# Softmax sums beside the values of an attention: two heads' values and ones in one stationary block, 32x32 transposes on VectorE, and another order of the streams

## The chip, the cores and the metric

The kernel runs on one core of a Trainium2 chip. The metric is the device time of one execution in microseconds; less is better. All data is float32.

## The reference, cut to what matters

Four transformer blocks are applied to `x` of shape (128, 64, 128): 128 batch elements, 64 tokens, 128 features. They hold five attentions with 16 heads of 8 features each, two MLPs and a last block with a router and three experts. The change touches only the attentions, whose core is:

```python
attn = jnp.einsum('bhnd,bhsd->bhns', q, k) * SCALE
attn = jax.nn.softmax(attn, axis=-1)
o = jnp.einsum('bhns,bhsd->bhnd', attn, v)      # 64 queries, 64 keys, 16 heads of 8
```

## The kernel before, in words

**Tiling.** Four batch elements make a group (`GROUP`), so there are 32 groups. Each group passes through all five attentions, which makes 160 attentions in a run. Five groups are in flight at a time, one in each stream (`STREAMS = 5`).

**What sets the order.** The steps of one group stand in `GROUP_STEPS`. The string `SEQUENCE` says, digit by digit, which stream makes its next step; `interleave()` turns it into `ORDER`. Every engine walks through the same `ORDER` and issues its own part of each step, in that order. Semaphores tie the engines together.

**Steps of an attention.** `q`, `k` and `v` are projections. `tops` computes scores once to find maxima, `lows` transposes the negated maxima, `scores` computes the scores again less the maximum. ScalarE takes the exponential of each of the four banks of scores (L1203, one for each `g`). The result is `pT[s]`, laid out as keys of two heads (64 partitions each) by (`g`, batch element `tb`, `lo`, query). `g` runs over four quads of heads.

**Sums and values on TensorE.** For `sums` (L874) a stationary block of ones and zeros with 32 columns, `own_ones`, adds up the exponentials over the keys. Each matmul has 256 moving columns, and there are 8 of them. For `values` (L887) the stationary block holds the values, and there are 32 matmuls of 64 moving columns. Both use a quarter of the array's columns for a matmul. Which quarter (strip) it is follows from the 32 partitions of the bank that the output goes to, `dst[QUAD * g:QUAD * (g + 1), ...]`. In both steps `g` is the innermost loop:

```python
for tb in range(GROUP):
    for lo in range(2):
        for g in range(TURNS):
            mm = nc.tensor.matmul(dst[QUAD * g:QUAD * (g + 1), tb * SEQ:(tb + 1) * SEQ], ...
```

The trace has two rows for each such float32 matmul, which are called passes here, and one or two for each weight load.

**On VectorE.** `sums` is inverted over all 128x256 elements (L1063). `values` is then multiplied by it (L1070) into `oT`, which the step `out` (L897) projects.

**Another step that the prediction speaks of.** `l3_evidence` (L945) makes two matmuls on rows 0 to 63 of the array and then two on rows 64 to 127. Its loop over the halves is the outer one.

**Banks.** Four PSUM banks form a ring that all projections, sums and values share. A step takes the next bank and waits until its last content has been moved out. The other four banks (`turns`) belong to `tops` and `scores`.

Of the kernel before, what the change touches and what calls it, by code (L numbers as in the profile page):

```python
# [7 lines left out]
ALU = mybir.AluOpType  # L8
# [6 lines left out]
D = 128  # L15
# [66 lines left out]
ALL_WEIGHTS = 16 * (3 + len(W_LOADS[1:]))  # L82
# [48 lines left out]
def attention(a):  # L131


    return [("q", a), ("k", a), ("v", a), ("tops", None), ("lows", None), ("scores", None),
            ("sums", None), ("values", None), ("out", a)]
# [6 lines left out]
def norm(eps, how):  # L142
# [26 lines left out]
    "0021100003030101012012311010100102000030112001100100111100100231000120000100101110312002110201201010"  # L169
    "0200210122012131012022100120200102021011012201032112312003230002213212302133202031230310321303024031"  # L170
    "0410301441203320203411101032132132443421143201143213401232244200302344230043320310041241134203120012"
    "4412232424012312033143420234413303224011042121003404103104032024013003210432434041431411143234234120"
    "1034332024031130241021413024012401214024431143230242003143201031044032431340320121423211434041422210"
    "3423043231241432201130322303241421430400220112340221143230132223300244011234043214101241040420103314"
    "3202433042311040412144340023210134110223101434210313242043401340313021203302403104103014412033202034"
    "1110103213213244342114320114321340123224420030234423004332031004124113420312001244122324240123120331"
    "4342023441330322401104212100340410310403202401300321043243404143141114323423412010343320240311302410"
    "2141302401240121402443114323024200314320103104403243134032012142321143404142221034230432312414322011"
    "3032230324142143040022011234022114323013222330024401123404321410124104042010331432024330423110404121"
    "4434002321013411022310143421031324204340134031302120330240310410301441203320203411101032132132443421"  # L180
    "1432011432134012322442003023442300433203100412411342031200124412232424012312033143420234413303224011"
    "0421210034041031040320240130032104324340414314111432342341201034332024031130241021413024012401214024"
    "4311432302420031432010310440324313403201214232114340414222103423043231241432201130322303241421430400"
    "2201123402211432301322233002440112340432141012410404201033143202433042311040412144340023210134110223"
    "1014342103132420434013403130212033024031041030144120332020341110103213213244342114320114321340123224"
    "4200302344230043320310041241134203120012441223242401231203314342023441330322401104212100340410310403"
    "2024013003210432434041431411143234234120103433202403113024102141302401240121402443114323024200314320"
    "1031044032431340320121423211434041422210342304323124143220113032230324142143040022011234022114323013"
    "2223300244011234043214101241040420103314320243304231104041214434002321013411022310143421031324204340"
    "1340313021203302403104103014412033202034111010321321324434211432011432134012322442003023442300433203"  # L190
    "1004124113420312001244122324240123120331434202344133032240110421210034041031040320240130032104324340"
    "4143141114323423412010343320240311302410214130240124012140244311432302420031432010310440324313403201"
    "2142321143404142221034230432312414322011303223032414214304002201123402211432301322233002440112340432"
    "1410124104042010331432024330423110404121443400232101341102231014342103132420434013403130212033402014"
    "3043041210131212314310221001424304123140020101300241003023401310342310224312413421343321431204340320"
    "4142033124403231021420320421432414112002430344033021340434210043030324211104203124140130423300231403"
    "4103110304403140341110041421201420441240213414132031042410304111404021424300401413240221143310410413"
    "1040112311102011241143014132034100401240110400101301420130411214001343401041403303110011130041111310"
    "104010310404311420301441101031410141100104120110341414401101311111113011"
# [15 lines left out]
def bank_uses(kind, arg):  # L215
# [5 lines left out]
        "lows": (0, 1), "sums": (1, 0), "values": (1, 0),  # L221
# [127 lines left out]
def build(nc, x, cond, context, weights, biases, rows, ident_in, own_head_in, own_ones_in, gate_store, out):  # L349
# [3 lines left out]
    with ExitStack() as ctx:  # L353
# [16 lines left out]
        own_ones = sb("own_ones_sb", [D, 2, QUAD])  # L370
# [22 lines left out]

        v_heads = each("v_heads", [D, GROUP * TURNS, 2 * QUAD])
        top = each("top", [D, D])
        inv_sum = each("inv_sum", [D, TOK])
        low = [i[:, 0:D] for i in inv_sum]
        oT = each("oT", [D, GROUP, SEQ])

# [132 lines left out]
        with nc.Block() as block:  # L532
# [23 lines left out]
            def _(pool):  # L556
# [3 lines left out]
                for s in range(STREAMS):  # L560

                    nc.gpsimd.memset(v_heads[s][:, :, :], 0.0).then_inc(consts_made, 1)
# [729 lines left out]
```

## Time and profile before

| | us |
|---|---|
| median of 3 runs | 2047.76 (2044.34 to 2049.5) |
| profiled execution, its own time | 2036.93 |
| span of the profiled execution | 2035.2 |
| TensorE (PE) busy | 1920.9 |
| weight loads (PEld) busy | 1591.5 |
| VectorE (DVE) busy | 1685.4 |
| ScalarE (ACT) busy | 1411.7 |
| GpSimd (POOL) busy | 648.7 |

The profiled execution is 10.8 us below the median of the runs. 1.7 us of it lie outside the span. Busy times of engines overlap each other, so they do not add up. Busy time of TensorE is the union of its passes, each of which has a modelled end.

### The profile page before, as it was taken

To read this page: it belongs to the slowest core of one execution; us is meant where nothing else is said; L and a number is where in the kernel's file an instruction comes from. 1 tells how busy PE (TensorE), PEld (TensorE's weight loads), DVE (VectorE), ACT (ScalarE), POOL (GpSimd) and SP (SyncE) were. 2 spreads that over 40 slices of the span, in tenths; PEclk is the share of its full clock that TensorE was granted. 3 is DMA by queue.
4 is the path that set the end of the run, shared out by engine and by line. 5 is a ranking of instruction groups with operands and counts; after the bars stand their busy time and mean duration, and the time that the engine had idled before them with its cause. 6 is when DMAs were issued, how large, how long until landed. Compare 5 with 4: busy or idle time off the path is not lost.

```text
span 2035.2 us, 93251 instructions
## 1 busy us (share of the span) xinstructions
PE 1920.9 (94%) x40741; PEld 1591.5 (78%) x40741; DVE 1685.4 (83%) x3915; ACT 1411.7 (69%) x3672; POOL 648.7 (32%) x1132
## 2 busy tenths in 40 slices
PE   3789999999999999999999999999999999999998
PEld 2567878887877887878887877887888887777877
DVE  2778888888888898878898888898888888889875
ACT  1455767777776777776777776777776777676777
POOL 1322333333333323333323333333333332323322
PEclk9899999999999999999999999999999999999999
DMA  4200000000000000000000000000000000000000
GB/s 176 53 3 3 16 21 21 21 11 18 21 16 21 21 21 11 19 16 21 21 20 10 20 16 21 21 21 21 9 16 21 21 21 8 21 16 8 3 3 14
DMA packets 48113, 42.97 MB, mean 21 GB/s; under 512 B 12640, under 2 KB 38368, under 8 KB 47456
## 3 DMA queue, kind: packets, MB, share of 16 engines
q1 hardware_dynamic: 47712, 37.02, 6.4%
q8 instruction: 326, 5.34, 1.1%
q14 instruction: 75, 0.61, 0.1%
HBM read 32.54 MB, written 4.46 MB: 18 GB/s over the span
## 4 chain that ended last, share of the span: by engine, by line
PE 79%; DVE 10%; ACT 6%; issue 2%; DMA 1%; POOL 0%; DVEq 0%; ACTq 0%; POOLq 0%
PE bank L967 9%; PE turns L858 8%; PE turns L841 7%; PE turns L862 7%; PE bank L874 6%; PE bank L887 6%; PE bank L904 5%; PE bank L914 5%; PE bank L976 4%; PE bank L897 3%; PE bank L812 3%; PE bank L779 3%; DVE top L1059 3%; PE bank L827 3%; PE bank L816 3%; ACT pT L1203 2%
## 5 line engine op out<-in xcount | busy, mean ns | idle before, releaser
L1203 ACT ACTIVATE pT<-turns 128x512 f32<-128x512 f32 x640 | 330.2, 602 | 165.1 <-PE turns L862 164.7
L738 POOL TENSOR_TENSOR shifted<-moments,eps 128x2 f32<-128x2 f32 x256 | 50.1, 196 | 1127.1 <-DVE moments L1023 1126.5
L1059 DVE TENSOR_REDUCE top<-turns 128x32 f32<-128x2048 f32 x160 | 364.2, 2276 | 44.3 <-PE turns L841 43.6
L1063 DVE RECIPROCAL inv_sum<-bank 128x256 f32<-128x256 f32 x160 | 279.7, 1748 | 39.7 <-PE bank L874 38.6
L858 PE MATMUL turns<-inv_sum,of_keys 32*128 32x128 f32 x5120 | 277.9, 284 | 3.8 <-issue 2.3
L862 PE MATMUL turns<-q_heads,k_heads 32*128 32x128 f32 x5120 | 263.0, 271 | 2.7 <-issue 2.6
L1238 ACT ACTIVATE pT<-bank,mod 128x64 f32<-128x64 f32 x896 | 195.7, 331 | 51.7 <-PE bank L967 50.6
L858 PEld LDWEIGHTS turns<-inv_sum,of_keys 32*128 32x128 f32 x5120 | 206.8, 187 | 30.5 <-ACT inv_sum L1152 13.1
L862 PEld LDWEIGHTS turns<-q_heads,k_heads 32*128 32x128 f32 x5120 | 209.2, 187 | 4.0 <-issue 3.8
L1029 DVE TENSOR_SCALAR n_rows<-x_rows,moments,rstd 128x128 f32<-128x128 f32 x512 | 185.6, 405 | 29.3 <-POOL rstd L740 28.2
L841 PE MATMUL turns<-k_heads,q_heads 32*128 32x128 f32 x5120 | 189.4, 283 | 12.5 <-ACT pT L1203 10.2
L1180 ACT ACTIVATE k_heads<-bank,key_bias,own_head_sb 128x256 f32<-128x256 f32 x320 | 164.3, 573 | 51.2 <-PE bank L816 51.1
L740 POOL TENSOR_TENSOR rstd<-shifted,minus_halves 128x2 f32<-128x2 f32 x256 | 187.1, 731 | 20.1
L887 PEld LDWEIGHTS bank<-pT,v_heads 128*32 128x32 f32 x10240 | 161.9, 110 | 36.6 <-issue 16.1
L841 PEld LDWEIGHTS turns<-k_heads,q_heads 32*128 32x128 f32 x5120 | 159.2, 186 | 39.6 <-issue 26.8
L1051 DVE TENSOR_SCALAR q_heads<-bank,b_sb,own_head_sb 128x256 f32<-128x256 f32 x320 | 156.5, 530 | 34.9 <-PE bank L812 34.4
L887 PE MATMUL bank<-pT,v_heads 128*32 128x64 f32 x10240 | 177.4, 220 | 8.0 <-issue 6.4
L874 PE MATMUL bank<-pT,own_ones_sb 128*32 128x256 f32 x2560 | 170.8, 383 | 4.9 <-ACT pT L1203 4.7
L1190 ACT ACTIVATE v_heads<-bank 64x128 f32<-64x128 f32 x640 | 138.6, 267 | 21.5 <-PE bank L827 19.2
L967 PE MATMUL bank<-nT,w_sb 128*128 128x256 f32 x448 | 137.2, 387 | 0.3 <-issue 0.3
L904 PE MATMUL bank<-nT,w_sb 128*128 128x256 f32 x512 | 135.3, 392 | 0.2
L1152 ACT ACTIVATE inv_sum<-bank 128x128 f32<-128x128 f32 x160 | 46.2, 289 | 126.8 <-PE bank L849 126.3
(150 smaller groups left out, 3923.1 us busy)
## 6 DMA issues: line engine op xcount, KB each, us to landing
gates<-gate_store SPq DMA_DIRECT2D x64, 256.0 KB, 4.2
x_rows<-x SPq DMA_DIRECT2D x32, 128.0 KB, 2.1
c_rows<-context SPq DMA_DIRECT2D x32, 128.0 KB, 2.1
out<-x_rows SPq DMA_DIRECT2D x32, 128.0 KB, 1.8
w_sb<-weights SPq DMA_DIRECT2D x1, 2368.0 KB, 12.6
pT<-weights SPq DMA_DIRECT2D x1, 1024.0 KB, 4.9
logit_bias<-logit_store SPq DMA_DIRECT2D x64, 1.5 KB, 3.4
row_sb<-rows SPq DMA_DIRECT2D x1, 769.5 KB, 6.7
```

What stands on the lines that cost most here:

```text
L740: nc.gpsimd.tensor_tensor(rstd[s][:, :], shifted[s][:, :], minus_halves[:, 0, :], ALU.pow).then_inc(rstd_in[s], 1)
L841: mm = nc.tensor.matmul(by_turn[g][:, tb * D:(tb + 1) * D], q_heads[s][part, tb, :, :], k_heads[s][part, tb, :, :], start=True, stop=True)
L858: nc.tensor.matmul(by_turn[g][:, tb * D:(tb + 1) * D], of_keys[part, 2 * tb:2 * tb + 2, :], low[s][part, :], start=True, stop=False)
L862: mm = nc.tensor.matmul(by_turn[g][:, tb * D:(tb + 1) * D], k_heads[s][part, tb, :, :], q_heads[s][part, tb, :, :], start=False, stop=True)
L874: mm = nc.tensor.matmul(dst[QUAD * g:QUAD * (g + 1), 0:TOK], own_ones[:, lo, :], pT[s][:, g, :, lo, :], start=lo == 0, stop=lo == 1)
L887: mm = nc.tensor.matmul(dst[QUAD * g:QUAD * (g + 1), tb * SEQ:(tb + 1) * SEQ], v_heads[s][:, tb * TURNS + g, lo * QUAD:(lo + 1) * QUAD], p ...
L904: mm = nc.tensor.matmul(dst[:, c * TOK:(c + 1) * TOK], w(layer["w1"], 0, 2 * half + c), nT[s][:, :, :], start=True, stop=True)
L967: mm = nc.tensor.matmul(dst[:, r * TOK:(r + 1) * TOK], weight, src[:, :, :], start=c == 0, stop=c == 1)
L1059: nc.vector.tensor_reduce(top[s][:, :].rearrange("p (g c) -> p g c", c=32)[:, :, 0:2 * GROUP], turns[:, :, :].rearrange("p g (c k) -> p g ...
L1063: nc.vector.reciprocal(inv_sum[s][:, :], banks.take()[:, 0:TOK]).then_inc(v_emptied, 1)
L1203: nc.scalar.activation(turn_cols[s][:, g, :], by_turn[g][:, :], ACT.Exp, scale=ATT_SCALE).then_inc(scores_read, 1)
L1238: m = nc.scalar.activation(dst, src[:, at], ACT.Silu, bias=mod[s][:, k, tb:tb + 1])
```

## The change

1. `sums` is gone as a step. The stationary block of `values` gets 32 columns for two heads: 8 columns of values of the first head, 8 of the second, 8 of ones on the first head's keys and 8 of ones on the second's. So a matmul gives values and sums. It no longer accumulates over `lo`; the output fills all 512 columns of a bank.
2. The loop over `g` becomes the outermost loop of `values`. It waits at each `g` for that exponential alone.
3. VectorE transposes the bank in 32x32 blocks, which brings queries to the partitions. It inverts 32 sums for each partition, multiplies 128x256, and transposes back.
4. ScalarE moves the values out of the bank in two instructions of 64x256 instead of four of 64x128. Columns of two masks change places for that, and `wv` is read in another order.
5. Ten memsets on GpSimd write the ones at the start; the load of `own_ones` is gone. The transposed rows are kept in `q_heads`.
6. `SEQUENCE` is another string of digits, with one step less for each attention.

```diff
@@ TensorE, steps of ORDER
-                    if kind == "sums":
-
-                        after("pT", s)
-                        dst = to_v.slot()
-                        for lo in range(2):
-                            for g in range(TURNS):
-                                mm = nc.tensor.matmul(dst[QUAD * g:QUAD * (g + 1), 0:TOK], own_ones[:, lo, :], pT[s][:, g, :, lo, :],
-                                                      start=lo == 0, stop=lo == 1)
-                        mm.then_inc(v_filled, 1)
+                    if kind == "values":
+
+                        after("v", s)
+                        dst = to_v.slot()[:, :].rearrange("p (b h l q) -> p b h l q", b=GROUP, h=2, l=2)
+                        for g in range(TURNS):
+                            pe.wait_ge(scores_read, ready["pT", s] + g + 1)
+                            for tb in range(GROUP):
+                                for lo in range(2):
+                                    mm = nc.tensor.matmul(dst[QUAD * g:QUAD * (g + 1), tb, :, lo, :], v_heads[s][:, 2 * (tb * TURNS + g) + lo, :],
+                                                          pT[s][:, g, tb, lo, :].rearrange("p (h q) -> p h q", h=2), start=True, stop=True)
                         mm.then_inc(v_filled, 1)
-                    if kind == "values":
-
-                        after("v", s)
-                        after("pT", s)
-                        dst = to_v.slot()
-                        ready["o", s] = to_v.moved_out()
-                        for tb in range(GROUP):
-                            for lo in range(2):
-                                for g in range(TURNS):
-                                    mm = nc.tensor.matmul(dst[QUAD * g:QUAD * (g + 1), tb * SEQ:(tb + 1) * SEQ],
-                                                          v_heads[s][:, tb * TURNS + g, lo * QUAD:(lo + 1) * QUAD], pT[s][:, g, tb, lo, :],
-                                                          start=lo == 0, stop=lo == 1)
-                        mm.then_inc(v_filled, 1)
@@ VectorE
-                    if kind == "sums":
-                        nc.vector.reciprocal(inv_sum[s][:, :], banks.take()[:, 0:TOK]).then_inc(v_emptied, 1)
-                        sums_at[s] = banks.uses
-
                     if kind == "values":
 
-                        src = banks.take()
-                        dve.wait_ge(v_emptied, sums_at[s])
-                        nc.vector.tensor_tensor(oT[s][:, :, :].rearrange("p g q -> p (g q)"), src[:, 0:TOK], inv_sum[s][:, :],
-                                                ALU.mult).then_inc(v_emptied, 1)
+                        nc.vector.transpose(weighed[s], banks.take()[:, :]).then_inc(v_emptied, 1)
+                        dve.wait_ge(v_emptied, banks.uses)
+                        by_query = weighed[s].rearrange("p (n c) -> p n c", c=4 * HD)
+                        own_result(nc.vector.reciprocal(inv_sum[s][:, :, :], by_query[:, :, 2 * HD:4 * HD:HD]))
+                        own_result(nc.vector.tensor_tensor(o_rows[s][:, :].rearrange("p (n a d) -> p n a d", a=2, d=HD),
+                                                           by_query[:, :, 0:2 * HD].rearrange("p n (a d) -> p n a d", a=2),
+                                                           inv_sum[s][:, :, :].unsqueeze(3).broadcast_to([D, GROUP * 4, 2, HD]), ALU.mult))
+                        nc.vector.transpose(oT[s][:, :, :].rearrange("p g q -> p (g q)"), o_rows[s][:, :]).then_inc(o_turned, 1)
@@ ScalarE
-                            for lo in range(2):
-                                at = lo * QUAD + (2 * pair + lo) * HD
-                                m = nc.scalar.activation(v_heads[s][part, :, at:at + HD],
-                                                         src[part, 0:TOK].rearrange("p (n l d) -> p n l d", l=2, d=HD)[:, :, lo, :],
-                                                         ACT.Identity)
+                            m = nc.scalar.activation(v_heads[s][part, :, HD * pair:HD * (pair + 1)],
+                                                     src[part, 0:TOK].rearrange("p (n d) -> p n d", d=HD), ACT.Identity)
@@ the order of the streams, first line of many
-    "0021100003030101012012311010100102000030112001100100111100100231000120000100101110312002110201201010"
+    "0101000002201010130311101002201130320030012001101010111200100310001300200100101101021102012010010200"
```

On TensorE, in the middle of the program, sums and values of one attention stand as two rows before, here one behind the other (L827 is a `v`, L841 a `tops`, L904 an MLP step):

```order
L904 MATMUL bank<-nT,w_sb 128x256 x2
L827 MATMUL bank<-w_sb,nT 32x64 x16
L874 MATMUL bank<-pT,own_ones_sb 32x256 x8
L887 MATMUL bank<-pT,v_heads 32x64 x32
L841 MATMUL turns<-k_heads,q_heads 128x128 x16
```

After the change TensorE has one row of 32 matmuls (L882), and five rows of other streams until the projection of this attention's result (L893):

```order
L882 MATMUL bank<-pT,v_heads 32x2x32 x32
L833 MATMUL bank<-w_sb,cT 32x64 x16
L847 MATMUL turns<-k_heads,q_heads 128x128 x16
L785 MATMUL bank<-ident_sb,n_rows 128x128 x2
L916 MATMUL bank<-nT,w_sb 128x256
L893 MATMUL bank<-w_sb,oT 128x128 x2
```

The eight matmuls of `own_ones` are gone; the 32 matmuls of the values are as many and as wide as they were (2x32 columns are 64), but their order by strip is that of the new loop.

On VectorE, in the middle of the program, before the change an attention of stream 2 has its inversion and its product with another stream's work between them:

```order
L1063 RECIPROCAL inv_sum2<-bank3 128x256
L1029 TENSOR_SCALAR n_rows3<-x_rows3,moments3,rstd3 128x128 x2
L1070 TENSOR_TENSOR oT2<-bank1,inv_sum2 128x256
```

After it, an attention of stream 0 has four instructions in a row, each of which needs the one before it:

```order
L1055 TENSOR_REDUCE top1<-turns 128x4x8
L1060 STREAM_TRANSPOSE q_heads0<-bank3 128x512
L1063 RECIPROCAL inv_sum0<-q_heads0 128x32
L1064 TENSOR_TENSOR o_rows0<-q_heads0,inv_sum0 128x256
L1067 STREAM_TRANSPOSE oT0<-o_rows0 128x256
```

Two instructions became four, and the wait for them lies in one piece.

## Rows read from the trace of the kernel before

**Rows 1.** The page's busy times: engine, us, share of the span, instructions.
```profile
PE 1920.9 (94%) x40741; PEld 1591.5 (78%) x40741; DVE 1685.4 (83%) x3915; ACT 1411.7 (69%) x3672; POOL 648.7 (32%) x1132
PEclk9899999999999999999999999999999999999999
```

**Rows 2.** The page's chain that ended last, by engine.
```profile
PE 79%; DVE 10%; ACT 6%; issue 2%; DMA 1%; POOL 0%; DVEq 0%; ACTq 0%; POOLq 0%
```

**Rows 3.** Stretches: us, busy time of PE, PEld, DVE, ACT, POOL; clock, DMA.
```profile
500.00:1000.00 500.00, 485.06 (x10508) 404.30 (x10504) 426.43 (x990) 363.98 (x942) 163.21 (x285) 1.00 0.07 18
1000.00:1500.00 500.00, 486.12 (x10547) 404.18 (x10545) 431.25 (x1000) 361.18 (x940) 167.76 (x292) 1.00 0.07 19
```

**Rows 4.** The chain in order of time: start us, us, what, passes.
```profile
1003.56 1.03 PE bank L887 x64
...
1016.43 1.00 PE bank L874 x16
1017.44 0.89 PE bank L887 x64
...
1020.76 0.45 PE bank L897 x4
...
1022.52 0.58 PE bank L827 x32
1023.11 0.86 PE bank L874 x16
1023.97 0.89 PE bank L887 x64
1024.86 1.10 PE turns L841 x32
```

**Rows 5.** Groups by line on PE: passes, busy us, mean ns, idle before.
```profile
L887 PE MATMUL bank<-pT,v_heads 128*32 128x64 f32 x10240 | 177.4, 220 | 8.0 <-issue 6.4 <-DVE inv_sum L1063 1.5
L874 PE MATMUL bank<-pT,own_ones_sb 128*32 128x256 f32 x2560 | 170.8, 383 | 4.9 <-ACT pT L1203 4.7
```

**Rows 6.** L945's first passes: stretches, PE busy (passes in it), PEld busy.
```profile
1001.40:1001.42 0.02, 0.01 (x1) 0.01 (x1) 1.00 0.00 0
1001.42:1001.43 0.01, 0.01 (x2) 0.01 (x2) 1.00 0.00 0
1001.56:1001.58 0.02, 0.02 (x3) 0.02 (x4) 1.00 0.00 0
1001.58:1001.60 0.02, 0.02 (x4) 0.02 (x4) 1.00 0.00 0
```

**Rows 7.** Timeline around 1001 to 1008 us: start, us, instruction, what ended the idle time.
```profile
1001.41 0.67 PE L945 MATMUL bank<-pT,c_rows 64*128 64x64 f32 x8
1002.10 0.45 ACT L1152 ACTIVATE pT<-bank 128x128 f32<-128x128 f32 x2 [0.42 <-PE bank L945]
...
1007.86 2.06 ACT L1203 ACTIVATE pT<-turns 128x512 f32<-128x512 f32 x4 [3.99 <-PE turns L862]
```

**Rows 8.** Groups by line on DVE: count, busy us, mean ns, idle before.
```profile
L1059 DVE TENSOR_REDUCE top<-turns 128x32 f32<-128x2048 f32 x160 | 364.2, 2276 | 44.3 <-PE turns L841 43.6
L1063 DVE RECIPROCAL inv_sum<-bank 128x256 f32<-128x256 f32 x160 | 279.7, 1748 | 39.7 <-PE bank L874 38.6
L1037 DVE TENSOR_TENSOR nT<-nT,mod 128x256 f32<-128x256 f32 x160 | 82.2, 514 | 5.5
L1070 DVE TENSOR_TENSOR oT<-bank,inv_sum 128x256 f32<-128x256 f32 x160 | 67.1, 419 | 20.0 <-PE bank L887 12.3 <-issue 0.2
L1116 DVE RECIPROCAL inv_r<-total_r 128x2 f32<-128x2 f32 x32 | 5.3, 166 | 1.1
L629 DVE COPY of_keys<-own_row 128x512 f32<-128x512 f32 x1 | 0.4, 427 | 0.0
```

**Rows 9.** Groups by line on ACT: count, busy us, mean ns, idle before.
```profile
L1190 ACT ACTIVATE v_heads<-bank 64x128 f32<-64x128 f32 x640 | 138.6, 267 | 21.5 <-PE bank L827 19.2
L1152 ACT ACTIVATE nT<-bank 128x256 f32<-128x256 f32 x64 | 24.7, 386 | 24.5 <-PE bank L779 23.7
```

**Rows 10.** Timeline of GpSimd at the start: start, us, instruction.
```profile
0.82 4.50 POOL L562 MEMSET v_heads<- 128x1024 f32 x5
46.92 0.19 POOL L738 TENSOR_TENSOR shifted<-moments,eps 128x2 f32<-128x2 f32 x1 [41.60 <-DVE moments L1023]
```

More of the change, by code:

```diff
@@ L134, in attention @@
     return [("q", a), ("k", a), ("v", a), ("tops", None), ("lows", None), ("scores", None),
-            ("sums", None), ("values", None), ("out", a)]
+            ("values", None), ("out", a)]
 def mlp(m):
@@ L174 @@
[L174 to L183, printed above, removed]
@@ new lines @@
+    "2440230124013403014421423204122321400142222014003341142034041322321340313132441434321210430143313002"
+    "4012124410041213430233023121013310114432033104143242201240043024324131402001433220410211203224403203"
+    "4201134414203231224341044301423100322144034421204113120433021401024031213203004104301214032214312314"
+    "4134231130001343240400244112203402341132031021243230210012103242433431013120430234203340021104140311"
+    "1431204031022403240231240412342332042334103201320114303244023012401340301442142320412232140014222201"
@@ L200 @@
+    "111001111111"
 )
@@ L220, in bank_uses @@
         "kvnorm": (1, 0) if modulated else (0, 1), "q": (1, 0), "k": (0, 1), "v": (0, 1),
-        "lows": (0, 1), "sums": (1, 0), "values": (1, 0),
+        "lows": (0, 1), "values": (1, 0),
         "out": (1, 0), "fc1": (0, 1), "fc2": (1, 0), "l3_query": (0, 1), "l3_scores": (1, 0),
@@ L392, in build @@
         q_heads, k_heads = each("q_heads", [D, GROUP, 2, SEQ]), each("k_heads", [D, GROUP, 2, SEQ])
-        v_heads = each("v_heads", [D, GROUP * TURNS, 2 * QUAD])
+        v_heads = each("v_heads", [D, GROUP * TURNS * 2, 4 * HD])
         top = each("top", [D, D])
-        inv_sum = each("inv_sum", [D, TOK])
-        low = [i[:, 0:D] for i in inv_sum]
+        o_rows = each("o_rows", [D, TOK])
+        inv_sum = each("inv_sum", [D, GROUP * 4, 2])
+        low = [o[:, 0:D] for o in o_rows]
+        weighed = [q[:, :, :, :].rearrange("p g l q -> p (g l q)") for q in q_heads]
         oT = each("oT", [D, GROUP, SEQ])
@@ L414, in build @@
         top3, total3, inv3 = each("top3", [D, 2]), each("total3", [D, 2]), each("inv3", [D, 2])
-        p3 = [i[:, 0:D].rearrange("p (t k) -> p t k", t=2) for i in inv_sum]
-        pn3 = [i[:, D:2 * D].rearrange("p (t k) -> p t k", t=2) for i in inv_sum]
+        p3 = [o[:, 0:D].rearrange("p (t k) -> p t k", t=2) for o in o_rows]
+        pn3 = [o[:, D:2 * D].rearrange("p (t k) -> p t k", t=2) for o in o_rows]
         p3T = in_turns(3, TOK, 2, SEQ)
@@ L562, in _ @@
                     nc.gpsimd.memset(v_heads[s][:, :, :], 0.0).then_inc(consts_made, 1)
+                for s in range(STREAMS):
+                    pool.wait_ge(consts_made, 3 + STREAMS + 2 * s)
+                    for pair in range(2):
+                        at = HD * (2 + pair)
+                        nc.gpsimd.memset(v_heads[s][SEQ * pair:SEQ * (pair + 1), :, at:at + HD], 1.0).then_inc(consts_made, 1)
             @block.tensor
@@ L990, in _ @@
                 count = Counted(dve)
-                banks, sums_at, attended = Emptier(dve, ring, FOR_VECTOR, v_filled), {}, 0
+                banks, attended = Emptier(dve, ring, FOR_VECTOR, v_filled), 0
                 def own_result(ins):
```

60 lines of the change are left out of this document (32 added, 28 removed).

## The prediction

> **What bounds the kernel now.** I read the busy times first. TensorE is busy for 1920.9 of 2035.2 us, VectorE for 1685.4 and ScalarE for 1411.7 [rows 1]. The chain that ended last then says who holds the end: 79% of it is TensorE's own work, VectorE has 10% and ScalarE 6% [rows 2]. Last I read stretches in the middle. In 500 us TensorE is busy for 485 to 486 and VectorE for 426 to 431, at a granted clock of 1.00, which is the upper level, 2.4 GHz [rows 3]. So TensorE stands idle for about 15 us in 500, some 60 us in the run without its start. The reader is to see that the program is bound by what TensorE has to do: an edit counts by the TensorE time that it adds or takes, and nothing else can give back more than those 60 us.
>
> **The sums go.** On the chain, where TensorE never stops, the step L874 takes 0.86 us (once) and 1.00 us (where the next step is of another kind) [rows 4]. I take 0.93 us. 160 attentions give 149 us less. Bounds: 138 and 160 us.
>
> **The values keep their count and change their order.** This is the term that decides. The 32 matmuls leave 64 passes, before as after. Before, the 64 passes take 0.89 us on the chain [rows 4], while one of them alone lasts 220 ns in the records [rows 5]; so many of them overlap. How many count as simultaneous is read from the pace. A pass of 128 columns over the whole array takes 0.45/4 = 0.112 us (L897) [rows 4], so 64 columns take 0.056 us. 0.89 us are 16 times 0.056 us. So each strip works through its own 16 passes at the pace of the whole array, and the four strips do so at the same time. The sums agree: 4 passes of 256 columns a strip, 4 x 0.224 = 0.90 us against 0.86 [rows 4].
>
> The new loop gives TensorE all 16 passes of strip 0, then all 16 of strip 1, and so on. Two passes of one strip cannot share it. If the strips took turns entirely, the step would last 64 x 0.056 = 3.56 us. What helps is that TensorE can let a pass overtake earlier ones that wait for another part of the array. How far it does that is seen at one place only, L945. Its code has four passes on the lower rows and then four on the upper. The rows show a second pass begun by 1001.43, and the third only at 1001.56 to 1001.58 [rows 6]. With passes of 64 columns on one half 0.056 us apart at least, the second one started belongs to the other half: it overtook three passes (and their weight loads) that stood before it. Both results also came out together: ScalarE, waiting for L945, moved both at 1002.10, after all eight passes of 0.67 us [rows 7]. So overtaking reaches three passes or more, and nothing in the trace shows how many more.
>
> With an overtaking of n passes the next strip starts when n passes of the present one are left to begin. The step then has 64 - 3n passes one after another, as long as n is at most about 10. n = 3 gives 55 passes, 3.06 us; n = 0 gives 3.56 us; n = 16 or more lets two whole strips run side by side, 1.78 us, and without any limit it is 0.89 us as before. I take n = 4, next to the only row: 52 passes, 2.89 us, which is 2.00 us more than now, 320 us in 160 attentions. I choose a small n because three is what is seen, and each further pass that stands aside needs room for itself and its load.
>
> The Trainium skill bears on this, in "TensorE: Matmul & The Clock Gate", Part 3, "The mechanism". It says that matmuls start and end strictly in the order of the program; only weight loads are pulled ahead. By that rule n is 0, and the sum would be 80 us above mine or more. The row on L945 speaks against it: there a matmul started before three earlier ones. The same section also speaks of a reorder window that is 64 deep. Counted in loads and matmuls this would be two strips of this step; nothing in these rows shows such a depth.
>
> **The new waits on TensorE.** `values` waits for one exponential at a time. The four of them last 2.06 us together [rows 7], 0.52 us each, and a strip takes 0.67 us (12 passes) or more; so once the first is there the later ones come in time. Behind the waiting instruction stand all streams' matmuls. Before, the same step waited for all four, and ahead of L887 only 8.0 us were idle in the run [rows 5]. I cost this at nothing; the old wait covers it.
>
> **VectorE.** Gone: 1748 + 419 ns [rows 8]. New: a transpose of 128x512 out of a bank, not shown by any row. The nearest rows are the copy of 128x512, 427 ns, and the reduction over 2048 columns of banks, 2276 ns or 1.11 ns a column, so 570 ns; as bounds I keep 0.43 us and, at the slowest pace of any row (the inversion, 6.8 ns a column), 3.5 us. I take 0.65 us. The inversion of 32 columns: (1748 - 166)/254 = 6.2 ns a column on top of 166 ns, so 0.35 us. The product with its broadcast operand is between 419 and 514 ns, I take 0.45. The transpose back of 128x256 I take at 0.40 us (bounds 0.3 and 1.75). Together 1.85 us against 2.17: VectorE is relieved by 0.3 us an attention, 51 us in all, down from 1685. It isn't the bound, so the sum gets nothing for that. On the transposes, the Trainium skill, "Vector Engine (DVE) Microarchitecture Reference", 3.8, gives one element a cycle for each lane, by which 512 columns would be an estimate of 0.53 us; no row here shows it.
>
> The path from the last pass of the values to `out` grows from 0.42 to about 1.9 us. In the rows of the new order a `v`, a `tops`, two transposes and a matmul of the experts stand between them: 0.58 + 1.10 us for the first two alone [rows 4], and more than 0.4 us for the rest. That hides it there; where less lies between, TensorE waits for up to 1 us.
>
> **The rest.** ScalarE's four moves of 267 ns become two of at most 386 ns [rows 9]: 0.3 us less, off the path. The added memsets follow five that end at 5.3 us, while GpSimd has nothing to do until 46.9 us [rows 10]; even 5 us of them would be hidden. One small load less before the start: nothing.
>
> **The idle time.** TensorE gets more work, VectorE and ScalarE less, and each attention has one step, one bank use and one change of array layout less. Of the 60 us some are given back; I take 20 (bounds 0 and 60). A worse stream order could cost as much.
>
> **Sum.** 2036.93 (profiled execution) - 149 + 320 - 20 = 2188 us. The median of the runs before lies 10.8 us above the profiled one, so 2199 us; I say 2198.
>
> **The rivals.**
> *Deep overtaking (ends faster).* TensorE lets a strip overtake 16 passes or more. Two strips at a time: 1.78 us a step, 160 x 0.89 = 142 more, 149 less, 20 given back: 2010, or 2021 as a median. All four at a time: 0.89 us, which gives 1868 and 1879. For it: the overtaking is real, and it is the same machine that keeps four strips full now. Against it: only three passes are shown. It decides from a step of 0.89 + 0.93 + 20/160 = 1.95 us, 35 passes, n of about 10. Chance 0.29. The reorder window of 64 in the skill's page is its sentence.
> *Strict order between strips.* n = 0: 3.56 us, 160 x 2.67 - 149 - 20 = +258, so 2306. Rows 6 speak against it. Chance 0.08. The skill's rule on strict order is its sentence.
> *VectorE late.* The transposes cost near their upper bound, or the longer path to `out` is not covered. If half of the attentions make TensorE wait for 1 us, 80 us come on top of the forecast: 2278. If a transpose of 128x512 took 3.5 us and one of 128x256 1.75, VectorE would need 6.05 us an attention instead of 2.17, 1685 + 620 = 2305 us, and be the bound. Chance 0.05.
> *The forecast* (n from 3 to about 7): 0.58, its own range 2110 to 2265.
>
> **How the numbers follow.** Slower by over 0.3% (about what a measurement of this kernel can tell from no change): 0.58 + 0.08 + 0.05 = 0.71, less 0.02 for a forecast whose n and idle time fall out so well that nothing is lost: 0.69. Of the deep rival's 0.29, 0.26 end faster and 0.03 within 0.3%, which makes 0.05 there. The range must leave out 2 in 10 at most: it takes the forecast's own range and goes down to two strips at a time, 1995 to 2268; outside are overtaking of all strips and strict order.
>
> **What would show it.** In the trace after: the values step (L882 x64) on the chain for about 2.9 us instead of 0.89, its busy time near 160 x 3.05 = 490 us, TensorE's busy share at 95% or more, VectorE at about 1630 us. If the step shows 1.8 us or less, the overtaking was mis-sized and the kernel is at par or faster. If it shows 3.5 us, there is none between strips. If VectorE is busy beyond 1900 us, or `out` waits for `oT` for more than 40 us in all, the VectorE part was wrong.

## The result, and the profile after

The changed kernel takes 2252.59 us, the median of 4 runs (2248.81 to 2257.74). The kernel before took 2046.5 us on the same chip (2044.34 to 2049.5). The ratio is 1.1008, with a 95% interval from 1.098 to 1.1035. The forecast was 2198 us. The profiled span grew from 2035.2 to 2249.8 us, by 214.6 us.

The page of the kernel after: busy times, granted clock, the chain that ended last by engine and by line. It answers to [rows 1, 2].

```profile
PE 2116.3 (94%) x38181; PEld 1847.0 (82%) x38181; DVE 1666.7 (74%) x4235; ACT 1400.8 (62%) x3346; POOL 655.2 (29%) x1142
...
PEclk8899999999999999999999999999999999999999
...
PE 80%; DVE 10%; ACT 5%; issue 2%; POOL 0%; DMA 0%; SPq 0%; ACTq 0%; DVEq 0%
PE bank L882 22%; PE bank L963 8%; PE turns L864 7%; PE turns L847 6%; PE turns L868 6%; PE bank L910 5%; PE bank L900 4%; PE bank L972 4%; DVE top L1055 4%; PE bank L818 3%; PE bank L822 3%; PE bank L785 3%; PE bank L893 3%; PE bank L833 3%; ACT pT L1196 2%
```

TensorE has 2560 passes less than before and is busy for 195 us more. VectorE and ScalarE are busy for less. The chain's shares by engine are within a point of those of before, and its first line is the values step, L882. So the bound is still TensorE, and one step of it became dear.

The groups of the kernel after by line, on PE and on DVE: passes or instructions, busy us, mean ns of one, idle time before them. They answer to [rows 5, 8].

```profile
L882 PE MATMUL bank<-pT,v_heads 128*32 128x64 f32 x10240 | 508.1, 220 | 0.5 <-ACT pT L1196 0.4
...
L1067 DVE STREAM_TRANSPOSE oT<-o_rows 128x256 f32<-128x256 f32 x160 | 71.3, 445 | 5.5
...
L1064 DVE TENSOR_TENSOR o_rows<-q_heads,inv_sum 128x256 f32<-128x256 f32 x160 | 70.8, 442 | 5.5
...
L1060 DVE STREAM_TRANSPOSE q_heads<-bank 128x512 f32<-128x512 f32 x160 | 114.7, 717 | 284.2 <-PE bank L882 284.2
...
L1063 DVE RECIPROCAL inv_sum<-q_heads 128x32 f32<-128x32 f32 x160 | 56.5, 353 | 5.4
```

The values had 177.4 us of TensorE before and have 508.1 now, with the same 10,240 passes of the same 220 ns. Only fewer of them overlap. VectorE waits 284.2 us for them, which costs nothing.

The chain in order of time shows one such step, and the one behind it (start, us, what, passes). It answers to [rows 4].

```profile
1013.30 0.43 PE bank L822 x2
1013.74 2.94 PE bank L882 x61
1016.68 0.04 PE bank L833 x3
1016.72 0.01 PE bank L882
1016.73 0.04 PE bank L833 x3
1016.78 0.01 PE bank L882
1016.79 0.04 PE bank L833 x3
1016.83 0.01 PE bank L882
1016.85 0.45 PE bank L833 x23
1017.29 1.92 PE bank L900 x8
```

61 passes take 2.94 us where 64 took 0.89 to 1.03 [rows 4]. The end shows the overtaking itself. L833 is the `v` of another stream, on all four strips. Three of its passes, on the free strips, start ahead of the third-last pass of L882, three more ahead of the second-last, and three more ahead of the last.

Four stretches that begin just ahead of this step show when its strips start. They count L882 alone; the number behind the first x is that of its passes begun so far:

```profile
1013.60:1014.35 0.75, 0.69 (x12) 0.69 (x13) 1.00 0.09 23
1013.60:1014.37 0.77, 0.70 (x14) 0.71 (x15) 1.00 0.08 22
1013.60:1015.05 1.45, 1.39 (x28) 1.39 (x29) 1.00 0.04 12
1013.60:1015.07 1.47, 1.41 (x30) 1.41 (x31) 1.00 0.04 12
```

Passes of one strip begin 0.056 us apart, its first two 0.08 us. Within 0.02 us the 13th and the 14th begin, and 0.70 us later the 29th and the 30th: each time one of the strip at work and the first of the next one.

The waits of TensorE in the kernel after: who waits, for whom, us in all, how many, the longest.

```profile
PE bank L855 <- DVE top L1055: 27.5, 37, 1.8
PE bank L785 <- DVE n_rows L1025: 20.4, 34, 2.2
PE turns L847 <- ACT pT L1196: 14.7, 23, 1.6
...
PE bank L893 <- DVE oT L1067: 5.1, 6, 2.1
```

L855 is `lows`, which waits for the maxima `top`; L785 are the transposes ahead of the projections, which wait for the normed rows `n_rows`; L847 is `tops`. The kernel before waited 11.3 us for `top` and 10.8 us for `n_rows`. The projection `out` (L893) hardly waits for its operand.

### The profile page after: what moved, and what is told of

It is laid out like the page before. It is cut to its first block, busy times and chain, and to the rows that moved or that the text cites. A ratio compares the mean times of both kernels' runs of the same rounds, so it can differ in the third digit from the quotient of the medians.

```text
span 2249.8 us, 87819 instructions
## 1 busy us (share of the span) xinstructions
PE 2116.3 (94%) x38181; PEld 1847.0 (82%) x38181; DVE 1666.7 (74%) x4235; ACT 1400.8 (62%) x3346; POOL 655.2 (29%) x1142
## 4 chain that ended last, share of the span: by engine, by line
PE 80%; DVE 10%; ACT 5%; issue 2%; POOL 0%; DMA 0%; SPq 0%; ACTq 0%; DVEq 0%
PE bank L882 22%; PE bank L963 8%; PE turns L864 7%; PE turns L847 6%; PE turns L868 6%; PE bank L910 5%; PE bank L900 4%; PE bank L972 4%; DVE top L1055 4%; PE bank L818 3%; PE bank L822 3%; PE bank L785 3%; PE bank L893 3%; PE bank L833 3%; ACT pT L1196 2%
## 5 line engine op out<-in xcount | busy, mean ns | idle before, releaser
L882 PEld LDWEIGHTS bank<-pT,v_heads 128*32 128x32 f32 x10240 | 484.4, 110 | 29.7 <-issue 24.3
L882 PE MATMUL bank<-pT,v_heads 128*32 128x64 f32 x10240 | 508.1, 220 | 0.5 <-ACT pT L1196 0.4
L1060 DVE STREAM_TRANSPOSE q_heads<-bank 128x512 f32<-128x512 f32 x160 | 114.7, 717 | 284.2 <-PE bank L882 284.2
L864 PE MATMUL turns<-o_rows,of_keys 32*128 32x128 f32 x5120 | 278.4, 287 | 8.6 <-ACT o_rows L1148 6.4
L864 PEld LDWEIGHTS turns<-o_rows,of_keys 32*128 32x128 f32 x5120 | 207.3, 190 | 43.7 <-ACT o_rows L1148 29.9
L847 PE MATMUL turns<-k_heads,q_heads 32*128 32x128 f32 x5120 | 189.4, 284 | 17.9 <-ACT pT L1196 14.7
L847 PEld LDWEIGHTS turns<-k_heads,q_heads 32*128 32x128 f32 x5120 | 159.9, 187 | 47.5 <-issue 20.8
L1184 ACT ACTIVATE v_heads<-bank 64x256 f32<-64x256 f32 x320 | 121.3, 379 | 94.8 <-PE bank L833 92.5
L1201 ACT ACTIVATE pT<-bank,b_sb 128x256 f32<-128x256 f32 x256 | 106.8, 471 | 85.2 <-PE bank L900 83.0
L1148 ACT ACTIVATE o_rows<-bank 128x128 f32<-128x128 f32 x160 | 45.3, 283 | 163.8 <-PE bank L855 163.1
L963 PE MATMUL bank<-nT,w_sb 128*128 128x256 f32 x448 | 140.0, 394 | 0.1
L963 PE MATMUL bank<-pT,w_sb 128*128 128x256 f32 x448 | 133.3, 379 | 0.0
```

The costliest lines, as they stand in the source:

```text
L847: mm = nc.tensor.matmul(by_turn[g][:, tb * D:(tb + 1) * D], q_heads[s][part, tb, :, :], k_heads[s][part, tb, :, :], start=True, stop=True)
L864: nc.tensor.matmul(by_turn[g][:, tb * D:(tb + 1) * D], of_keys[part, 2 * tb:2 * tb + 2, :], low[s][part, :], start=True, stop=False)
L882: mm = nc.tensor.matmul(dst[QUAD * g:QUAD * (g + 1), tb, :, lo, :], v_heads[s][:, 2 * (tb * TURNS + g) + lo, :], pT[s][:, g, tb, lo, :].re ...
L963: mm = nc.tensor.matmul(dst[:, r * TOK:(r + 1) * TOK], weight, src[:, :, :], start=c == 0, stop=c == 1)
```

## The experiments

Each kernel was timed against the kernel before on the same chip. Ratios are to that kernel, with their 95% intervals. Its median beside the different runs lay between 2044.0 and 2049.0 us, so a difference between two changed kernels is uncertain by some 5 us.

**The order of the loops, alone: e1_inner.** The changed kernel with `g` innermost again, and so one wait for all four exponentials:

```diff
-                        for g in range(TURNS):
-                            pe.wait_ge(scores_read, ready["pT", s] + g + 1)
-                            for tb in range(GROUP):
-                                for lo in range(2):
+                        pe.wait_ge(scores_read, ready["pT", s] + TURNS)
+                        for tb in range(GROUP):
+                            for lo in range(2):
+                                for g in range(TURNS):
```

> The changed kernel with g as the innermost loop of the values step again, and one wait for all four exponentials ahead of it. Strip theory (TensorE loses the overlap of the four strips, because 16 passes of one strip stand in a row): the step falls from 2.94 us on the chain to about 0.9, 160 x 2.04 = 326 us less, so about 1925 us; with waits that TensorE's work covered until now, 1925 to 1965, faster than the kernel before. Rival (the loss comes from VectorE's four-instruction chain or from the order of the streams): the step's own time falls too, but TensorE then waits for oT and for banks instead, and the time stays above 2046.

Measured: 2001.18 us (1998.77 to 2003.69), ratio 0.978 (0.9737 to 0.9823). This loop with its waits is worth 251 us, and the rest of the change makes the kernel 2.2% faster than before. Its page, its group of L882, two waits and one piece of its chain:

```profile
PE 1808.0 (90%) x38181; PEld 1522.5 (76%) x38181; DVE 1661.4 (83%) x4235; ACT 1397.7 (70%) x3346; POOL 658.7 (33%) x1142
```
```profile
L882 PE MATMUL bank<-pT,v_heads 128*32 128x64 f32 x10240 | 176.6, 220 | 43.0 <-ACT pT L1196 33.7 <-DVE q_heads L1047 5.9 <-DVE n_rows L1127 1.4
```
```profile
PE bank L882 <- ACT pT L1196: 33.7, 60, 1.6
PE bank L855 <- DVE top L1055: 32.8, 44, 2.0
```
```profile
1011.27 0.89 PE bank L882 x64
```

The step takes 0.89 us again where it is shortest (1.10 us in the median of its pieces on the chain) and its group 176.6 us. From the step's start to the next step's start it fell by 323 us in the run, as expected. The result lies above the expectation because TensorE's idle time rose by 57.7 us. Most of that is the 43.0 us ahead of this step, mostly for exponentials, where the kernel after waits 0.5 us.

**How long may a run on one strip be: e2_fours, e3_eights, e4_pairs.** All three have the single wait of e1_inner, except that e4_pairs has one for each pair. e1_inner gives a strip 1 matmul (2 passes) before the next strip's turn, e2_fours 2 matmuls (4 passes), e3_eights 4 (8 passes); the kernel after has 8 (16 passes). In e4_pairs two strips take turns, 2 passes each, and then the other two. In e3_eights and e4_pairs the values' matmul stands one line lower, at L883.

```diff
# e2_fours
+                        for tb in range(GROUP):
+                            for g in range(TURNS):
+                                for lo in range(2):
# e3_eights
+                        for pair_tb in range(2):
+                            for g in range(TURNS):
+                                for tb in range(2 * pair_tb, 2 * pair_tb + 2):
+                                    for lo in range(2):
# e4_pairs
+                        for two in range(2):
+                            pe.wait_ge(scores_read, ready["pT", s] + 2 * two + 2)
+                            for tb in range(GROUP):
+                                for lo in range(2):
+                                    for g in range(2 * two, 2 * two + 2):
```

> As e1_inner, but four passes of a strip stand in a row (loops tb, g, lo). Short-overtaking theory (the next strip starts together with the fourth-last pass of the present one, three are overtaken): a run of four passes is short enough, each strip starts at once, 16 to 18 pass times of 0.056 us a step, 0.9 to 1.0 us, so within 10 us of e1_inner. Rival (any second pass in a row on one strip costs): two matmuls in a row halve the overlap, some 1.8 us a step, 140 us above e1_inner.

Measured: 2004.76 us, ratio 0.9797 (0.9743 to 0.9852), the same as e1_inner within the noise. L882 is busy for 186.9 us, 10 more than there, or 0.06 us a step.

> As e1_inner, but eight passes of a strip stand in a row (loops over two halves of tb, then g, tb, lo). Short-overtaking theory: the next strip starts 4 pass times later, the second round of strip 0 when strip 3 has four passes left; 36 to 37 pass times, 2.0 to 2.07 us a step, 160 x 1.1 = 180 us above e1_inner, about 2110 to 2140. Deeper reordering (16 passes or more could be overtaken if they had room, and the 2.94 us have another cause): 0.9 to 1.65 us a step, under 120 us above e1_inner.

Measured: 2181.18 us, ratio 1.066 (1.0597 to 1.0722), 180 us more than e1_inner. That is the difference expected; only the base was higher. The step is a little longer than expected: from the first pass's start to the last one's it takes 2.16 to 2.19 us in all 160 steps. The group and two pieces of the chain of e3_eights:

```profile
L883 PE MATMUL bank<-pT,v_heads 128*32 128x64 f32 x10240 | 382.4, 222 | 42.9 <-ACT pT L1197 35.1 <-DVE q_heads L1048 6.3 <-DVE n_rows L1128 1.4
```
```profile
1006.39 2.20 PE bank L883 x64
...
1026.48 2.17 PE bank L883 x61
```

> As the changed kernel, but strips go in pairs: strips 0 and 1 alternate, then 2 and 3; a wait for two exponentials ahead of each pair. Short-overtaking theory: two strips at a time, 16 pass times a pair, the second pair starting with the fourth-last: 28 to 29 pass times, 1.6 us a step, 160 x 0.7 = 112 us above e1_inner, about 2040 to 2075. Rival (not the strips, but the early waits make the step long): as slow as the changed kernel.

Measured: 2041.63 us, ratio 0.997 (0.995 to 0.9991), 40 us more than e1_inner instead of 112. The group and a piece of the chain of e4_pairs say why:

```profile
L883 PE MATMUL bank<-pT,v_heads 128*32 128x64 f32 x10240 | 288.2, 221 | 0.9 <-DVE n_rows L996 0.6 <-ACT pT L1197 0.2
```
```profile
1025.53 1.59 PE bank L883 x64
```

The passes are busy for 112 us more than in e1_inner, as expected. But the idle time ahead of them falls from 43.0 to 0.9 us, since the first pair no longer waits for the exponentials of the second. In the whole run TensorE's busy time rose by 87.6 us over e1_inner and its idle time fell by 49.8, which gives the 38 us by which the span grew. Runs of 4 passes cost 0.06 us a step, 8 cost 1.3 us, 16 cost 2.1 us. An overtaking without limit (the deep rival) would have made all these equal.

**The early waits apart from the loop: e5_one_wait.** The changed kernel and its loop, with one wait for all four exponentials.

```diff
+                        pe.wait_ge(scores_read, ready["pT", s] + TURNS)
                         for g in range(TURNS):
-                            pe.wait_ge(scores_read, ready["pT", s] + g + 1)
```

> The changed kernel, g outermost as it is, but one wait for all four exponentials ahead of the first strip. In e1_inner TensorE stood idle for 43 us ahead of the values step, mostly for ScalarE's exponentials. Theory that the waits by g hide the exponentials: 30 to 60 us are lost, 2280 to 2310. Rival (they hide nothing in a step that lasts 3 us): within 10 us of the changed kernel's 2253.

Measured: 2302.97 us, ratio 1.1258 (1.1219 to 1.1297), 50 us over the kernel after. Its group:

```profile
L882 PE MATMUL bank<-pT,v_heads 128*32 128x64 f32 x10240 | 508.2, 221 | 42.6 <-ACT pT L1196 34.8 <-DVE q_heads L1047 6.4 <-DVE n_rows L1127 1.4
```

The waits by `g` are worth 50 us in this order of the streams, and they leave the 508 us as they are.

**The loop in the kernel before: e6_before_outer.** Only the values' loops of the kernel before are put in another order; sums, VectorE's part and `SEQUENCE` are its own.

```diff
-                        for tb in range(GROUP):
-                            for lo in range(2):
-                                for g in range(TURNS):
+                        for g in range(TURNS):
+                            for tb in range(GROUP):
+                                for lo in range(2):
```

> The kernel before, with one part of the change alone: g becomes the outermost loop of its values step (sums, waits, order of the streams as before). Strip theory: 2.0 us more a step, 320 us, less up to 40 us of idle time: 2325 to 2370. Rival (the strips matter only in the merged block, which writes a whole bank): under 100 us more.

Measured: 2328.08 us, ratio 1.1381 (1.1342 to 1.1419), 281 us more. Its group and a piece of its chain:

```profile
L887 PE MATMUL bank<-pT,v_heads 128*32 128x64 f32 x10240 | 506.7, 220 | 0.3 <-issue 0.3
```
```profile
1008.76 2.97 PE bank L887 x64
```

So neither the block of values and ones, nor the missing accumulation, nor the new order of the streams is needed for the loss. This change of three lines loses more by itself than the whole change did.

**The order of the streams: e7_old_order, e8_inner_old_order, e9_before_new_order, e10_inner_later.** e7 is the changed kernel with the order of before without the turns of `sums`; e8 is e1_inner with that order; e9 is the kernel before with the new order, sums directly ahead of values; e10 is e1_inner with about 60 of the values steps later. One line of digits of each:

```diff
# e7_old_order, e8_inner_old_order, the first line
-    "0101000002201010130311101002201130320030012001101010111200100310001300200100101101021102012010010200"
+    "0021100003030101012012311101001020000301200110100111100100231000120000001011103120211020120101000021"
# e9_before_new_order, the first line
-    "0021100003030101012012311010100102000030112001100100111100100231000120000100101110312002110201201010"
+    "0101000002201010130311100100220113032003001120011001010111200100310001300200110010110100211020120100"
# e10_inner_later, the second line
-    "1201201121021201020122001020211130021002121321032300232123201132032100221130230322144034421204113120"
+    "1201201121021201020122000120211130021002121321032300223123201132032100221130230322144034421204113120"
```

> The changed kernel with the order of the streams of before, from which only the sums steps are left out. Theory that part of the loss beyond the strips (about 50 us more than the steps alone explain) is the new order: 2190 to 2225. Rival (the order doesn't matter once TensorE is full): within 10 us of 2253.

Measured: 2311.16 us, ratio 1.1298 (1.126 to 1.1337): 58 us over the kernel after. TensorE waits 40.9 us for `oT`, where it waited 5.1.

> e1_inner with the order of the streams of before, less the sums steps. There more of other streams' work lies between scores and values, so one wait for all four exponentials costs little. Theory (sums gone at 0.93 us each, nothing else lost): 2046 less 149 is 1897, with the VectorE chain or other waits coming up 1900 to 1960, faster than e1_inner. Rival (the new order fits the merged step better, above all the longer way from values to out): slower than e1_inner's 2001.

Measured: 2088.11 us, ratio 1.0209 (1.018 to 1.0238): 87 us over e1_inner. TensorE's waits in it:

```profile
PE bank L893 <- DVE oT L1067: 63.9, 59, 2.2
PE bank L855 <- DVE top L1055: 48.9, 74, 2.0
```

The theory that the new order is a part of the loss has fallen. In e8_inner_old_order only 6.9 us are idle ahead of the values, as expected, but the old order leaves too little between values and `out` for the four VectorE instructions; the new one leaves enough.

> The kernel before with the changed kernel's order of the streams; each sums step stands right ahead of its values step. Theory that the new order is made for the merged step (a longer way from values to out, a shorter one from scores to values) and costs the old kernel its cover for the exponentials: TensorE idle 40 us or more ahead of the sums, 2075 to 2110. Rival (the new order is better or equal for both): 2047 or less.

Measured: 2136.21 us, ratio 1.0456 (1.0429 to 1.0483), more than expected. TensorE waits 35.9 us for the exponentials ahead of `sums`, which before had 4.7 [rows 5]. So of the two kernels the new order fits only the changed one.

> e1_inner, with some 60 of the 160 values steps moved behind a few steps of other streams, until about 2.3 us of TensorE's work lie between scores and values (if at least about 2 us are left to out). Theory (e1_inner loses 43 us because the values step waits for the exponentials): 15 to 35 us less than e1_inner, 1966 to 1986. Rival (the wait only moves to out or lows, which then come too early): within 8 us of 2001, or more.

Measured: 2033.13 us, ratio 0.9953 (0.9935 to 0.997): 32 us over e1_inner, not less. Three waits of e10_inner_later:

```profile
PE bank L855 <- DVE top L1055: 37.2, 51, 2.0
...
PE bank L893 <- DVE oT L1067: 17.2, 22, 2.2
...
PE bank L882 <- ACT pT L1196: 12.1, 17, 1.6
```

The wait for exponentials fell from 33.7 to 12.1 us, and the waits for `oT` and for `top` grew, the first from 5.6 to 17.2 us. The three together fell, from 72.1 to 66.5 us. But others came up: `tops` (L847) waits 8.8 us for `k_heads` instead of 0.2, and L916 waits 6.4 us for VectorE's first transpose, for which it did not wait. In all, TensorE's idle time rose from 191.2 to 207.3 us and its busy time by 12 us, which makes up the 28 us by which the profiled span grew. What was taken from one wait came back in others, with 16 us on top; why the busy time rose stays open. Moving this step later, by itself, doesn't pay.

**VectorE's four instructions: e11_no_chain, e12_inner_no_chain.** In the kernel after and in e1_inner two copies take their place. The division by the sums and the turning of the blocks are left out.

```diff
-                        nc.vector.transpose(weighed[s], banks.take()[:, :]).then_inc(v_emptied, 1)
+                        src = banks.take()
+                        nc.vector.tensor_copy(oT[s][:, :, :].rearrange("p g q -> p (g q)"), src[:, 0:TOK]).then_inc(v_emptied, 1)
                         dve.wait_ge(v_emptied, banks.uses)
...
+                        nc.vector.tensor_copy(inv_sum[s][:, 0:1, 0:1], oT[s][:, 0:1, 0:1]).then_inc(o_turned, 1)
```

> The changed kernel without VectorE's chain: a copy of 128x256 and one of a single element take the place of transpose, inversion, product and transpose (division and turning are left out). Theory (the chain is hidden at out, but 1.96 us in one piece delay the reductions of tops and the norms, on which TensorE waits): 15 to 35 us less than the changed kernel, 2218 to 2238. Rival (VectorE has nothing to do with the loss): within 8 us of 2253. Second rival (it is the main loss): over 100 us less.

Measured: 2232.84 us, ratio 1.0929 (1.0904 to 1.0954): 20 us under the kernel after, or 16 by the two ratios. VectorE is busy for 1465.5 us. TensorE's wait for `top` is 17.1 us instead of 27.5:

```profile
PE bank L855 <- DVE top L1055: 17.1, 13, 1.8
```

> The same cut in e1_inner. There TensorE covers less, so the chain shows more: 30 to 60 us less than e1_inner, 1940 to 1970. Rival: within 8 us of 2001.

Measured: 1980.81 us, ratio 0.9695 (0.9673 to 0.9717): 20 us under e1_inner (17 by the ratios), less than expected. The wait for `top` falls from 32.8 to 21.2 us; that for exponentials stays at 33.8. So the four instructions cost 16 to 20 us. Some 10 to 12 of it is the wait for the maxima behind them, and 4 the wait for `oT`. The wait for `n_rows` did not fall (20.4 and 23.7 us in the kernel after and in e11_no_chain). TensorE's busy time fell too, by 9.4 and 6.3 us; the profiled executions without the four instructions had less of the lower clock level (means of 0.992 for 0.988, 0.989 for 0.987), so that part need not be their doing. They are not what makes TensorE wait for the exponentials.

## Why the prediction was right, and where it was off

**What bounds the kernel: right.** TensorE's passes decide. Without VectorE's four instructions the time changed by 20 us, with the loop by 251.

**The values step: right, and shown.** The forecast was 52 pass times, 2.89 us on the chain; the shortest piece there takes 2.94 us for 61 passes, and the median of all 160 is 2.99. Busy time was forecast at about 490 us and came to 508.1. In the 160 steps the strips start 0.70 us apart in the median, and a strip starts 6 ns after the 13th of the 16 passes of the strip ahead. So the next strip starts when four passes are left, of which one has just begun: three are overtaken, as at L945. 3 x 0.70 + 0.90 gives 3.0 us. The three passes counted on their own would have given 3.06 us, n = 4 gave 2.89; the measured value lies between. The runs of 8 bear the same rule out: in e3_eights the strips start 0.25 us apart in all 160 steps, after 5 of the 8 passes have begun, and 7 x 0.25 + 0.45 gives the 2.2 us of its chain. With 4 in a row there is almost nothing to lose by it, and 0.9 us remain. That pieces of the chain are longer in some steps (up to 2.40 us in e3_eights) is not another pace of the strips; the starts of the passes are the same there.

**The rivals.** Deep overtaking fell by L882 and by e3_eights; the step would have to take 1.78 us or 0.89. Strict order fell too: it would give 3.56 us. The Trainium skill, "TensorE: Matmul & The Clock Gate", Part 3, "The mechanism", has matmuls start in program order; the nine passes of L833 that start ahead of the last ones of L882 disagree. The window of 64 in the same section disagrees as well, if it is read as a reach of matmuls past a busy strip: here it ended at three. VectorE late: the transposes cost 0.717 and 0.445 us, above the 0.65 and 0.40 that I took but far from 3.5 and 1.75, and `out` waited 5.1 us.

**The sums' end: right.** Sums and values together, from each step's start to the next step's, took 326.6 us before and 488.1 after: +161.5, where 320 - 149 = 171 were forecast. The sums had 148.2 us of it, forecast 149. The values went from 178.4 to 488.1, +309.7 for 320. That this difference is so near is in part luck: a step of the values took 1.11 us before and 3.05 after by this count, and I had put both too low, by 0.22 and 0.16 us. One reading was wrong without harm: I took a sums step of 1.00 us for one whose next step is of another kind, but both rows of L874 have L887 behind them [rows 4]. What differs is the step ahead: at 0.86 us it is L827, with 32 columns as well, at 1.00 us it is L849, with 128.

**The waits by `g`: right in amount, wrong in reason.** I wrote that the old wait covers them. The old wait covered them in the old order. In the new order one wait for four exponentials leaves 42.6 us idle (e5_one_wait) and costs 50 us. It is the wait by `g` itself that keeps them hidden. So the same loop costs 251 us against e1_inner as a net of about 300 us for overlap lost and 50 us for waits avoided.

**VectorE: near.** 1.85 us were forecast, 717 + 353 + 442 + 445 = 1957 ns were measured, as busy time 1666.7 us against 1630. The path to `out` was covered as forecast, but only thanks to the new order: the old one gives 40.9 and 63.9 us of waits (e7, e8). That the four instructions hold up `top` was not in the sum; it is 10 to 12 us.

**The step that failed: "the idle time", where 20 us were given back.** All steps but sums and values took 53 us more, not 20 less. I had argued that less work for VectorE and ScalarE and one step less mean fewer waits; the bounds were 0 and 60 us given back, and the sign was wrong. That is 73 us above the forecast; values and sums lay 10 below it, and the profiled span grew by 63 us more than the sum of the terms (214.6 against 151). The medians grew by 206 us; 2252.59 is 55 us above the 2198 forecast and 15 below the end of the range. The largest parts by kind of step, again from start to start: the transposes ahead of projections +21.6 us, `out` +12.1, `q` +11.1, `lows` +6.3, `k` +5.0, the experts' hidden layer (L967 before, L963 after) +4.7, scores -7.4. Three parts can be read:
- TensorE's span less its busy time went from 114.3 to 133.5 us. Idle time behind passes of sums and values, which the 161.5 us contain, fell from 13.7 to 2.1; so in the other steps it rose by 31 us. The waits for `top` and `n_rows` rose by 16.2 and 9.6 us. The four instructions stand in one piece of 2 us ahead of other streams' maxima, and e11_no_chain, without them, waits 10.4 us less for `top`; the 17.1 us that are left are near the 18.0 of e9_before_new_order, the kernel before with the new order. They do not explain `n_rows`: TensorE waits 23.7 us for it in e11_no_chain, and 19.6 in e9_before_new_order.
- The granted clock has a mean of 0.994 before and 0.988 after. At half speed in the lower level (1.2 GHz) that is 0.006 x 2035.2 x 2 = 24 us before and 0.012 x 2249.8 x 2 = 54 us after. The 30 us more cost at most half of that, 15 us. This need not come from the change: the kernel before had means from 0.987 to 0.994 in its other executions, and its profiled one is at the upper end; the four of the kernel after have 0.988 to 0.992.
- The rest of the 53 us, 22 us, is busy time of the other steps, of which the clock explains at most the 15. At least 7 us are left. The number of changes between kinds of array layout is nearly the same (1127 before, 1111 after), so they are not it. This part stays open.

**What is still there to be had.** e1_inner, the change with `g` innermost, takes 2001 us. It is faster than both kernels, by 2.2% and by 11%. Sums had 170.8 us of passes [rows 5]; TensorE's busy time fell by 1920.9 - 1808.0 = 112.9 us, and its idle time rose from 114.3 to 1999.2 - 1808.0 = 191.2, by 76.9 us. That leaves 36 us of span. 35.0 of the 76.9 are ahead of the values (8.0 to 43.0), 21.5 are waits for `top` (11.3 to 32.8), of which e12_inner_no_chain gives 11.6 back. That busy time fell by 58 us less than the passes of `sums` had is in part a matter of counting: these passes overlap their neighbours', and from start to start `sums` had 148.2 us, 23 less. The other 35 us are not settled.

## What to carry to other kernels

Where small float32 matmuls share the array by strips, the loop over the strips belongs innermost: runs of 4 passes on one strip cost 0.06 us, which the time does not show, 8 and 16 cost 1.3 and 2.1 us a step of 64. A wait by parts that needs the other loop order has a price that can be read from the chain and a gain that only a run with one wait shows; here it was 300 against 50 us. An order of streams fits the lengths of the chains for which it was found: with the wrong one the same kernel lost 58 or 87 us.

## What the runs showed of the hardware that was not expected

- Overtaking goes across steps: passes of the next step on free strips start ahead of the last passes of the present step (L833 between L882, 9 of them ahead of the last one). In all 160 steps of the kernel after and of e3_eights the strips start at the distance at which a pass overtakes three waiting ones, and not more; whether it is a count of passes or of places that passes and weight loads share is not settled.
- The inversion has a steep price by column (1748 ns for 256, 353 ns for 32), so that dividing after a transpose saves 1.4 us of VectorE; the two transposes, 717 + 445 ns, take most of that back.
- The lower clock level lasted for some 30 us longer in the profiled execution of the kernel after, 20 of them in the first 200 us. The executions of one kernel differ as much (means of 0.987 to 0.994 in the kernel before), so no run shows that the change has to do with it.
